# Keeping bf16 copies of the weights in HBM from the first token block on

## The reference

```
x = x + layernorm(attn(layernorm(x)))       # x is (4, 4096, 2048)
x = x + layernorm(ffn(layernorm(x)))

attn: q = x @ Wq; k = x @ Wk; v = x @ Wv    # 16 heads of 128
      s = (q k^T) * tril                    # masked with zeros
      softmax(s / 64) v, then @ Wo
ffn:  g = (x @ gate_w^T) * gate_s           # gate_w, up_w are (5632, 2048)
      u = (x @ up_w^T) * up_s
      ((silu(g) * u) @ down_w^T) * down_s   # down_w is (2048, 5632)
```

## Time and profile before

| what | us |
|---|---|
| median of 2 runs | 8050.35 (8044.33 to 8056.37) |
| the profiled execution | 7783.32 |
| its span, slowest core (core 5) | 7781.7 |
| spans of the 8 cores | 7729.8 to 7781.7 |
| busy in the span: PE / VectorE / ScalarE / GpSimd | 5885.8 / 2212.0 / 1647.7 / 815.4 |

### The profile page before, as it was taken

One profiled execution on the slowest core, in us unless ns is written; L12 is line 12 of the kernel. 1 busy time (PEld: TensorE's weight loads), 2 busy tenths in 40 slices (PEclk: granted clock), 3 DMA queues, 4 the chain that ended last, 5 costly groups with the idle time before them and its releaser, 6 DMA issues.

```text
span 7781.7 us, 66324 instructions; the slowest of 8 cores (7729.8 to 7781.7 us)
## 1 busy us (share of the span) xinstructions
PE 5885.8 (76%) x22048; PEld 2033.5 (26%) x22048; DVE 2212.0 (28%) x3308; ACT 1647.7 (21%) x2785; POOL 815.4 (10%) x1108
## 2 busy tenths in 40 slices
PE   7789999888778654886786648868875488878854
PEld 2244444322223221221232211112322111123321
DVE  5600000066230004662200056623000376530002
ACT  3311111144110002541000025511000155410000
POOL 0000000011011120110111101100111001001111
PEclk8899999988988997888999968888999788899898
DMA  3232222333347553223565432234765322236653
GB/s 89 85 66 60 52 58 65 109 86 84 68 78 111 87 76 111 69 72 68 87 109 89 68 111 69 72 68 65 111 93 73 110 58 64 69 52 108 105 73 65
DMA packets 476531, 625.15 MB, mean 80 GB/s; under 512 B 25648, under 2 KB 402480, under 8 KB 468016
## 3 DMA queue, kind: packets, MB, share of 16 engines
q0 software_dynamic: 345280, 402.72, 32.0%
q1 hardware_dynamic: 84848, 176.22, 7.3%
q10 hardware_dynamic: 46080, 41.96, 1.6%
HBM read 897.63 MB, written 58.72 MB: 123 GB/s over the span
## 4 chain that ended last, share of the span: by engine, by line
PE 63%; DMA 21%; DVE 10%; issue 4%; SPq 2%; ACT 1%; DVEq 0%; POOLq 0%; ACTq 0%
PE pb L218 63%; DMA dbig<-dwT 9%; DMA ubig<-uwT 3%; DMA gbig<-gwT 3%; DMA wob<-wo 3%; DVE rows_a L224 3%; DVE t L224 3%; SPq L212 2%; DVE y_all L224 1%; DMA xc<-xT 1%; DMA qh<-qscr 1%; DVE ao_all L224 1%; DVE xln L224 0%; DVE z_all L224 0%; DVE rows_b L224 0%
## 5 line engine op out<-in xcount | busy, mean ns | idle before, releaser
L224 DVE SCALAR_TENSOR_TENSOR sm<-pb,mask 128x512 f32<-128x512 f32 x1664 | 1123.6, 689 | 1619.7 <-PE pb L218 1580.3
L230 ACT ACTIVATE pt<-sm 128x512 bf16<-128x512 f32 x1664 | 1038.1, 630 | 585.2 <-DVE sm L224 581.7
L218 PE MATMUL pb<-h_all,dbig 128*128 128x512 bf16 x2816 | 698.4, 393 | 529.7 <-DMA dbig<-dwT 503.4
L218 PE MATMUL pb<-qh,kh 128*128 128x512 bf16 x1664 | 692.0, 446 | 184.8 <-DMA qh<-qscr 178.6
L218 PE MATMUL pb<-z_all,gbig 128*128 128x512 bf16 x2816 | 706.9, 413 | 164.9 <-DMA gbig<-gwT 148.5
L218 PE MATMUL pb<-z_all,ubig 128*128 128x512 bf16 x2816 | 696.9, 410 | 154.1 <-DMA ubig<-uwT 154.1
L218 PE MATMUL pb<-xln,wres 128*128 128x512 bf16 x3072 | 664.9, 380 | 32.9 <-DMA wres<-wk 32.9
L218 PE MATMUL pb<-pt,vh 128*128 128x512 bf16 x1664 | 662.6, 398 | 4.3 <-ACT pt L230 3.9
L218 PE MATMUL pb<-pt,ones_bf 128*1 128x512 bf16 x1664 | 649.9, 391 | 0.0
L224 DVE SCALAR_TENSOR_TENSOR h_all<-pb,us_sb,sg 128x512 bf16<-128x512 f32 x176 | 119.9, 744 | 1514.3 <-PE pb L218 1514.3
L218 PEld LDWEIGHTS pb<-h_all,dbig 128*128 128x128 bf16 x2816 | 259.5, 100 | 968.6 <-issue 736.2
(11 more groups left out here) (57 smaller groups left out, 3426.1 us busy)
## 6 DMA issues: line engine op xcount, KB each, us to landing
gbig<-gwT POOLq DMA_DIRECT2D x176, 512.0 KB, 7.0
ubig<-uwT POOLq DMA_DIRECT2D x176, 512.0 KB, 7.2
dbig<-dwT POOLq DMA_DIRECT2D x352, 256.0 KB, 4.0
kh<-kscr SPq DMA_DIRECT2D x64, 1024.0 KB, 5.9
vh<-vscr POOLq DMA_DIRECT2D x256, 256.0 KB, 7.7
xc<-xT SPq DMA_DIRECT2D x16, 2048.0 KB, 11.2
mask<-maskT SPq DMA_DIRECT2D x4, 8192.0 KB, 48.3
wob<-wo POOLq DMA_DIRECT2D x128, 256.0 KB, 4.0
```

The lines of the kernel that those rows point to most:

```text
L218: return E.matmul(o, l, rr, start=st, stop=sp)
L224: return getattr(E, n)(*a, **k)
L230: return getattr(E, n)(*a, **k)
```

## The change

Four tensors are added in each core's HBM, bf16 and laid out as the inputs: `woc`, `gwc`, `uwc` and `dwc`. In the first token block (`tb == 0`) each weight piece is loaded from its float32 input as before; once it has landed, a second DMA, issued from ScalarE's queue, writes the tile to its place in the copy. The next load of that buffer waits for this write too. In the token blocks 1 to 3 the pieces are loaded from the copies, still by DMAs that GpSimd issues, into the same tiles; there is no conversion then. The first two loads of each kind in token block 1 wait for the last writes of both buffers. The writes have eight semaphores of their own. Everything else is as it was.

Gate, as an example of the four (the others are alike):

```diff
+        ("woc", [D, D], BF16, "Internal"),
+        ("gwc", [D, 5632], BF16, "Internal"),
+        ("uwc", [D, 5632], BF16, "Internal"),
+        ("dwc", [5632, D], BF16, "Internal"),
...
                 gl = W(ev_gbig_user[bg])
                 if ig == 0 and ii < 2:
                     gl.append(ev_aall_war)
+                gsrc = d["gwT"] if tb == 0 else d["gwc"]
+                gl += W(ev_gwcw[bg] if tb == 0 else None)
+                if tb == 1 and ig == 0 and ii < 2:
+                    gl += W(ev_gwcw[0], ev_gwcw[1])
                 ev_gl = dma(c, "gpsimd", f"qg{bg}",
                             c.gbig[bg][:].rearrange("p (jj o) -> p jj o", jj=4),
-                            d["gwT"].ap().rearrange("(j p) o -> p j o", p=128)[
+                            gsrc.ap().rearrange("(j p) o -> p j o", p=128)[
                                 :, ii * 4:(ii + 1) * 4, ig * 512:(ig + 1) * 512],
                             waits=gl)
+                if tb == 0:
+                    ev_gwcw[bg] = dma(c, "scalar", f"qwg{bg}",
+                                      d["gwc"].ap().rearrange("(j p) o -> p j o", p=128)[
+                                          :, ii * 4:(ii + 1) * 4, ig * 512:(ig + 1) * 512],
+                                      c.gbig[bg][:].rearrange("p (jj o) -> p jj o", jj=4),
+                                      waits=[ev_gl])
```

More of the change, by code:

```diff
@@ L433, in record_program @@
     ev_wob_user = [None, None]
+    ev_wocw = [None, None]
+    ev_gwcw = [None, None]
+    ev_uwcw = [None, None]
+    ev_dwcw = [None, None]
     ev_gbig_user = [None, None]
@@ L582, in record_program @@
                     wl.append(ev_phaseA_pe)
+                wsrc = d["wo"] if tb == 0 else d["woc"]
+                wl += W(ev_wocw[bwo] if tb == 0 else None)
+                if tb == 1 and oh == 0 and i < 2:
+                    wl += W(ev_wocw[0], ev_wocw[1])
                 ev_wol = dma(c, "gpsimd", f"qo{bwo}", c.wob[bwo][:],
-                             d["wo"].ap()[i * 128:(i + 1) * 128,
-                                          oh * 1024:(oh + 1) * 1024], waits=wl)
+                             wsrc.ap()[i * 128:(i + 1) * 128,
+                                       oh * 1024:(oh + 1) * 1024], waits=wl)
+                if tb == 0:
+                    ev_wocw[bwo] = dma(c, "scalar", f"qwo{bwo}",
+                                       d["woc"].ap()[i * 128:(i + 1) * 128,
+                                                     oh * 1024:(oh + 1) * 1024],
+                                       c.wob[bwo][:], waits=[ev_wol])
                 for j in range(8):
@@ L701, in record_program @@
                     ul.append(ev_rows3)
+                usrc = d["uwT"] if tb == 0 else d["uwc"]
+                ul += W(ev_uwcw[bu] if tb == 0 else None)
+                if tb == 1 and ig == 0 and ii < 2:
+                    ul += W(ev_uwcw[0], ev_uwcw[1])
                 ev_ul = dma(c, "gpsimd", f"qu{bu}",
                             c.ubig[bu][:].rearrange("p (jj o) -> p jj o", jj=4),
-                            d["uwT"].ap().rearrange("(j p) o -> p j o", p=128)[
+                            usrc.ap().rearrange("(j p) o -> p j o", p=128)[
                                 :, ii * 4:(ii + 1) * 4, ig * 512:(ig + 1) * 512],
                             waits=ul)
+                if tb == 0:
+                    ev_uwcw[bu] = dma(c, "scalar", f"qwu{bu}",
+                                      d["uwc"].ap().rearrange("(j p) o -> p j o", p=128)[
+                                          :, ii * 4:(ii + 1) * 4, ig * 512:(ig + 1) * 512],
+                                      c.ubig[bu][:].rearrange("p (jj o) -> p jj o", jj=4),
+                                      waits=[ev_ul])
                 for jd in range(4):
@@ L745, in record_program @@
                     dl.append(ev_ln3_pe)
+                dsrc = d["dwT"] if tb == 0 else d["dwc"]
+                dl += W(ev_dwcw[bd] if tb == 0 else None)
+                if tb == 1 and og == 0 and ii < 2:
+                    dl += W(ev_dwcw[0], ev_dwcw[1])
                 ev_dl = dma(c, "gpsimd", f"qd{bd}",
                             c.dbig[bd][:].rearrange("p (jj o) -> p jj o", jj=2),
-                            d["dwT"].ap().rearrange("(j p) o -> p j o", p=128)[
+                            dsrc.ap().rearrange("(j p) o -> p j o", p=128)[
                                 :, ii * 2:(ii + 1) * 2, og * 512:(og + 1) * 512],
                             waits=dl)
+                if tb == 0:
+                    ev_dwcw[bd] = dma(c, "scalar", f"qwd{bd}",
+                                      d["dwc"].ap().rearrange("(j p) o -> p j o", p=128)[
+                                          :, ii * 2:(ii + 1) * 2, og * 512:(og + 1) * 512],
+                                      c.dbig[bd][:].rearrange("p (jj o) -> p jj o", jj=2),
+                                      waits=[ev_dl])
                 for jd in range(2):
```

1 line of the change is left out of this document (removed), and 2 rows, old and new, of the table DMAQ.

## The result

The changed kernel took 7723.59 us (median of 13 runs, 7521.56 to 7847.44) against 8039.76 us for the kernel before (10 runs, 7791.94 to 8138.34). In many runs of either kernel the cores of one die, or of both, show a lower granted clock and a longer span, and the ratio is taken from the runs without that: 0.963, 95% interval 0.952 to 0.974. The forecast was 7831 us, a ratio of 0.973, with a range of 7640 to 8070. The runs of either kernel spread over some 300 us, and both profiled executions lie in the lower part of theirs; the 267 us between the profile before and the first median are a matter of this spread.

The account below looks back on a forecast made before the run. TensorE waiting on weight-load DMAs was taken as the bound. Gains of 346 us in blocks 1 to 3 (231 gate/up, 84 down, 31 Wo) less 127 cost in block 0 gave 8050 - 219 = 7831 us, range 7640 to 8070.

Parts of the forecast that it names:

- The waits and the slow clock behind them: Gate/up, blocks 1 to 3: 66 gaps each 2.0 us shorter, 131 us, plus 100 of slow clock; together 231 us.
- the 100 taken as slow clock given back: Gate/up, blocks 1 to 3: of 119 us lost to the lower clock behind long gaps, 100 returns.
- Down and Wo in blocks 1 to 3: Each piece gains 0.32 us from faster loads: 84 us over 264 down pieces, 31 over 96 Wo pieces.
- I take 69 ns: Price of one bf16 packet in loads of blocks 1 to 3: gate piece 3.9 us after GpSimd's part, down piece 2.8.
- the rival by bytes: Load time follows source bytes read: gate piece 3.44 us, down piece 2.3; net -359 us, 7691 us; chance 0.25.
- down's price was taken over: Wo, blocks 1 to 3: down's gain of 0.32 us a piece applied to 96 pieces, 31 us.
- the premise that the count of packets stays: Loads before and after: a gate piece is 32 packets for each of 16 rings, a down piece 16.
- Block 0, gate/up: Copy writes cost gate/up in token block 0 5.8 us a block, by 11: 64 us, bounds 22 to 145.
- the step that was to cost most: Gate/up, block 0: writes of up pieces 0 and 1 wait behind four silu activations, 2.42 us; load 2 starts 2.0 later.
- The shared rings and the write's wait: Down, block 0: wait adds 0.36 us a round, ring sharing 0.69; 0.53 a piece by 88 is 46 us.
- packets decide: Loads on GpSimd's software queue cost by the packet; no gain, block 0 pays for writes: +200, 8250 us; chance 0.11.
- little comes of it: Only the slow tail of loads goes, gate 4.46 us and down 3.1: net -88 us, 7962 us; chance 0.24.

Follow-up runs that it names:

- the fp16 kernel: Changed kernel, but down in blocks 1 to 3 loads the bf16 copy into fp16 tiles, still converting; loads landed in 3.1 us, down took 275, 266, 271 us.
- those above: Changed kernel with only block 0's down writes altered (256 KB no wait, 128 KB, 4 KB, 4 KB no wait): down there 387, 376, 359, 316 us.

## Why the prediction was right, and where its terms were off

**The waits and the slow clock behind them.** Right in mechanism and nearly in size: gate's load 3.84 us where 3.9 was forecast, the gap 1.68 for 1.7, and gate/up in blocks 1 to 3 gained 214 us for 231. PE's busy time there fell by 89 us, for the 100 taken as slow clock given back.

**Down and Wo in blocks 1 to 3.** Undersized: 122 us for 84 and 75 for 31. The step that failed in down is the price of a bf16 packet, "I take 69 ns": a load takes 2.53 us after GpSimd and not 2.8, near the 2.3 of the rival by bytes, and half of 3.44 - 2.53 over 264 pieces is 120 us. In Wo it is that down's price was taken over: its load fell from 4.0 us to 2.8, 0.6 a piece or 58 us over 96 pieces, and PE's busy time fell from 207 to 190 us as the clock rose from about 0.90 to 0.97, slow clock given back for which the sum had no term. For the bytes, the fp16 kernel shows the same landing with and without conversion. Wrong too was the premise that the count of packets stays: in gate/up of block 1 GpSimd's queue has 12,544 packets for the 45.62 MB that took 45,952, since unconverted rows go several to a packet. The fp16 kernel shows no time gained by it.

**Block 0, gate/up.** 38 us for 64, and the step that was to cost most is wrong. The up writes do not stand behind the four silu activations:

```profile
2485.77 6.42 PE L223 MATMUL pb<-z_all,ubig 128*128 128x512 bf16 x29
2486.08 0.69 ACT L235 ACTIVATE sg<-pb,gs_sb 128x512 f32<-128x512 f32 x1 [38.85 <-DMA ubig<-uwT]
2486.41 0.37 ACTq L217 DMA_DIRECT2D uwc<-ubig  x1
2486.67 0.68 ACT L235 ACTIVATE sg<-pb,gs_sb 128x512 f32<-128x512 f32 x1
2487.03 0.37 ACTq L217 DMA_DIRECT2D uwc<-ubig  x1
...
2490.16 0.75 POOL L217 DMA_DIRECT2D ubig<-uwT  x1 [15.03 <-DMA uwc<-ubig]
```

(The window ends inside the first row's group, which has 32 matmuls.) The first up write is issued 0.33 us after the first silu begins, with three silu to come; the load of up piece 2 follows at 2490.16, 0.9 us after PE left piece 0, where the forecast had 2.6. What is left of the cost I put down to the traffic: float32 loads land in 7.9 and 8.4 us for 7.0 and 7.2, in a stage whose rings are busy 96% of the time in place of 68%. No run takes it apart, as those above do for down. The writes were mis-sized too: those of gate pieces landed in 8.0 us and those of up pieces in 5.4, for 2.83. Little of that reached the path of this block: the load of gate piece 2 was issued 0.84 us after PE had left piece 0, where it was 0.62 before.

**Block 0, down.** 87 us for 46. The shared rings and the write's wait were priced each for itself and added; the runs show that the traffic suffices and that the wait adds little to it (387 and 393 us), and leave open what the wait does alone. The term that was missing is the clock: 47 of the 87 us are matmuls at the lower clock behind gaps of about 3 us. I had given back slow clock where gaps shrink, but charged none in down, where they grow. Wo cost 26 for 17, the same way: PE's busy time there grew from 68 to 84 us. The Trainium skill's formula (DMA: Bandwidth & Descriptors, "Anatomy of one DMA") has the write of a down piece at an estimated 2.6 us, and the trace agrees: 2.6 for dwc, where the forecast had 2.15. The page gives it for DMAs that GpSimd issues, though, and these are ScalarE's, and for the gate and up pieces, where it gives an estimated 3.2 us, the trace has the 8.0 and 5.4 us above.

**The rivals.** That packets decide is refuted by the fp16 kernel, whose down loads kept their 23,392 packets a stage and landed in 3.1 us for 4.0; blocks 1 to 3 of the change do not refute it by themselves, since their packets fell too. That little comes of it is refuted by the landings, 3.84 and 2.53 us for the 4.46 and 3.1 of that rival. Bytes read decide for the load, as the fp16 kernel shows, and the loads of blocks 1 to 3 lie between forecast and that rival, which is why the result (-3.7%) lies between 7831 and 7691 us as ratios (-2.7% and -4.5%). That the total came out so near owes something to luck: the gain was 17 us too high in gate/up and 38 and 44 too low in down and Wo, the cost 26 too high in gate/up and 41 and 9 too low in down and Wo, so 65 us too little gain stood against 24 too little cost.

## What to carry to other kernels

A load that each use of a two-buffer loop waits for is worth its source bytes: a copy in the narrow type pays where it is read three times, and pays most if it is made in a stage whose rings are idle, a piece at a time and not in bursts. Where PE waits, count the length of the gaps and not only their sum: the same waiting in fewer, longer gaps also costs the clock. Loads that no longer convert need not be issued by GpSimd.

## What the runs showed that I had not expected

- Unconverted loads on GpSimd's queue are grouped: 12,544 packets for 45.62 MB where the converting ones need 45,952.
- GpSimd makes the descriptors of a 512 KB piece in 0.53 us when each partition has one run of 4 KB, in 0.74 with four of 1 KB.
- A DMA in ScalarE's list behind four activations went out 0.33 us after the first of them began.
- Writes of 4 KB that nobody waits for cost the down stage some 14 us; 256 KB with no wait, 85. (Waited for, 4 KB cost 57, in an execution whose lower clock may hold a part of it.)
- Copies from HBM to HBM in bursts of 21 held up 128 KB stores of another queue by up to some 40 us; one per three tiles of the projections, with four store buffers, cost no time that the trace shows.
